# Retention part of a fused kernel: the last tile in another order, and four low parts of the feed-forward made on VectorE ahead of the last block's gating

## What is computed

```python
for i in range(N_LAYERS):                       # 2 layers
    ln_x = layer_norm(x, ln1_g[i], ln1_b[i])
    q, k, v, xo = split(ln_x @ proj_w[i] + proj_b[i])
    ret = (q k^T * decay) v                     # 16 heads of 16, causal
    ret = (ret * silu(xo)) @ reto_w[i] + reto_b[i]
    x = x + ret
    h = layer_norm(x, ln2_g[i], ln2_b[i])
    x = x + gelu(h @ ffn1_w[i] + ffn1_b[i]) @ ffn2_w[i] + ffn2_b[i]
return layer_norm(x, lnf_g, lnf_b)              # then added to the stream before the part
```

## Time and profile before

| what | value |
|---|---|
| median of 3 runs | 1531.19 us |
| the 3 runs | 1527.48, 1531.32, 1531.19 us |
| time of the profiled execution | 1527.78 us |
| its span in the profile | 1525.9 us |
| busy: TensorE, VectorE, ScalarE, GpSimd | 1339.6, 1028.3, 596.3, 648.9 us |
| mean granted clock of TensorE over the span | 0.95 of full speed |

### The profile page before, as it was taken

One profiled execution on the slowest core, in us unless ns is written; L12 is line 12 of the kernel. 1 busy time (PEld: TensorE's weight loads), 2 busy tenths in 40 slices (PEclk: granted clock), 3 DMA queues, 4 the chain that ended last, 5 costly groups with the idle time before them and its releaser, 6 DMA issues. The chain is left out here.

```text
span 1525.9 us, 30606 instructions
## 1 busy us (share of the span) xinstructions
PE 1339.6 (88%) x11824; PEld 1098.0 (72%) x11824; DVE 1028.3 (67%) x2359; ACT 596.3 (39%) x1006; POOL 648.9 (43%) x508
## 2 busy tenths in 40 slices
PE   3899998478999999999998999999998637999993
PEld 2479995267888887887887887887787524699962
DVE  5854664768777777867767777877775377556634
ACT  6335664213343334234344233334333345266630
POOL 4765505524232232424334342543461455755045
PEclk9899999779999999999999999999999868999997
DMA  9987757500000000000010000000000051577544
GB/s 335 360 273 253 242 169 228 177 15 1 2 1 2 1 2 2 1 2 32 12 56 2 1 15 2 16 15 2 15 15 1 14 194 45 186 247 235 189 151 138
DMA packets 109323, 139.18 MB, mean 91 GB/s; under 512 B 11776, under 2 KB 95616, under 8 KB 109184
## 3 DMA queue, kind: packets, MB, share of 16 engines
q1 hardware_dynamic: 94784, 101.56, 20.4%
q0 software_dynamic: 12288, 33.57, 6.6%
q10 hardware_dynamic: 2112, 2.10, 0.4%
HBM read 71.66 MB, written 65.54 MB: 90 GB/s over the span
## 5 line engine op out<-in xcount | busy, mean ns | idle before, releaser
L1603 DVE TENSOR_TENSOR l_probs<-l_banks,l_past 128x512 f32<-128x512 f32 x256 | 159.9, 681 | 33.9 <-PE l_banks L1793 33.6
L1462 POOL TENSOR_TENSOR l_g_lo<-l_q,l_g_hi 128x1024 fp32r<-128x1024 f32 x16 | 53.8, 3361 | 266.3 <-ACT l_g_hi L1377 266.3
L79 PE MATMUL l_w_ps<-l_w_hi,l_f_hi 128*128 128x256 f32 x512 | 152.5, 298 | 15.7 <-DVE l_f_lo L1634 13.9
L1386 ACT ACTIVATE l_act_f<-l_w_ps,l_ffn_b 128x512 f32<-128x512 f32 x128 | 88.2, 689 | 190.6 <-PE l_w_ps L81 184.5
L80 PE MATMUL l_w_ps<-l_w_lo,l_f_hi 128*128 128x256 f32 x512 | 145.8, 285 | 0.0
L81 PE MATMUL l_w_ps<-l_w_hi,l_f_lo 128*128 128x256 f32 x512 | 145.7, 285 | 0.0
L79 PE MATMUL l_w_ps<-l_b_hi,l_w_hi 128*128 128x512 f32 x256 | 110.3, 431 | 13.4 <-POOL l_b_lo L1458 13.4
L79 PEld LDWEIGHTS l_w_ps<-l_w_hi,l_f_hi 128*128 128x128 f32 x512 | 99.0, 193 | 25.2 <-DVE l_f_lo L1634 23.0
L1634 DVE TENSOR_TENSOR l_f_lo<-l_act_f,l_f_hi 128x512 fp32r<-128x512 f32 x128 | 98.6, 818 | 18.1 <-ACT l_f_hi L1387 18.1
L597 POOL DMA_INDIRECT a_picked<-rows,a_pos_i x64 | 64.3, 1005 | 90.8 <-issue 69.5
L81 PE MATMUL l_w_ps<-l_b_hi,l_w_lo 128*128 128x512 f32 x256 | 102.0, 398 | 0.0
(11 more groups left out here) (376 smaller groups left out, 4022.1 us busy)
## 6 DMA issues: line engine op xcount, KB each, us to landing
rows<-a_zeros SPq DMA_DIRECT2D x15, 1024.0 KB, 12.6
a_xb<-rows SPq DMA_DIRECT2D x46, 256.0 KB
rows<-a_yb SPq DMA_DIRECT2D x46, 256.0 KB, 3.1
b_xb<-rows SPq DMA_DIRECT2D x46, 256.0 KB, 3.3
rows<-b_yb SPq DMA_DIRECT2D x46, 256.0 KB, 2.6
a_w_in<-in_moe_w SPq DMA_DIRECT2D x15, 384.0 KB, 12.7
b_w_in<-in_moe_w SPq DMA_DIRECT2D x15, 384.0 KB, 8.4
l_w<-in_ffn_w SPq DMA_DIRECT2D x8, 512.0 KB, 6.9
```

Of the source, the lines that this page charges most:

```text
L79: tensor.matmul(out, w_hi, x_hi, start=start, stop=False)
L1386: nc.scalar.activation(act_f[:, f, :], w_ps[:, f % 2, :], ACT.Gelu, bias=ffn1_b[:, b.layer, f:f + 1]).then_inc(act_done, 1)
L1603: dve.tensor_tensor(probs[c % 2][:, r * w:(r + 1) * w].rearrange("p (h n) -> p h n", n=P), banks[:, r, :].rearrange("p (h n) -> p h n", n= ...
```

## The change

Two things are changed.

First, in every step with a tile before it, block 3 of VectorE makes `f_lo` pieces 3, 4, 5 and 6 before `gate_result`, and only piece 7 behind it.

Second, the end is in another order. In step 15 TensorE does the first of the four groups of `feed_out` before `project_out`, then two groups, `turn_b`, and the last group. VectorE measures and normalises tile 13 before it adds the retention, and makes `b_lo` itself (`low_b` leaves GpSimd's list in this step, where it stood behind `finish` of tile 13). For tile 15 the hidden products go to the `banks` of PSUM and the four groups of `feed_out` to four banks of their own (`w_ps` and `rm_ps`). The tail of tile 15 is then done per block of 128 tokens: `measure_last(s)` and `finish_last(s)`. The final scale, shift and old stream are folded into two operations, for which GpSimd adds the shift to the old stream beforehand (`last_old`, loaded into `xn2` behind `turn_b`).

The diff, cut to its core:

```diff
+        def hidden_ps(b, f):
+            return banks[:, f % 2, :] if b.n == final.n else w_ps[:, f % 2, :]
+
+        def fed_ps(b, s):
+            return (w_ps[:, s, 0:D] if s < 2 else rm_ps[:, s - 2, 0:D]) if b.n == final.n else feed_ps[:, s, :]
@@ sync
-                with sp.Fori(1, NT) as t:
+                for t in range(1, NT - 1):
                     sp.wait_ge(final_done, t)
                     sp.dma_start(x_old[:, :, :], view[t]).then_inc(x_old_in, 16)
+                sp.wait_ge(bT_done, final.n + 1)
+                sp.dma_start(last_old[:, :, :], view[NT - 1]).then_inc(last_old_in, 16)
@@ scalar, step
                         root("f", after(b, -1))
-                        root("f", b)
+                        _, mv, std = norms["f"][:3]
+                        for s in range(SUB):
+                            act.wait_ge(last_var, s + 1)
+                            nc.scalar.activation(std[:, s:s + 1], mv[:, s, 1:2], ACT.Sqrt, bias=eps[:, :]).then_inc(last_std, 1)
...
                     if more == 0:
+                        root("f", after(b, -1))
                         root("2", a)
-                        root("f", after(b, -1))
@@ gpsimd, step
                     if a is None:
+                        pool.wait_ge(last_old_in, 16)
+                        carry(3)
+                        pool.tensor_tensor(last_old[:, :, :], last_old[:, :, :], normf[:, 1:2, :].broadcast_to([P, SUB, D]),
+                                           ALU.add).then_inc(last_old_done, 1)
                         finish(after(b, -1))
...
-                    low_b(a)
+                    if more:
+                        low_b(a)
@@ vector
+                def measure_last(s):
+                    stats, mv = norms["f"][:2]
+                    dve.wait_ge(last_fed, s + 1)
+                    dve.wait_ge(fed, final.n + 1)
+                    link(dve.tensor_tensor(tile_of(final, s), tile_of(final, s), fed_ps(final, s), ALU.add))
+                    dve.memset(carrier[:, 3:4], 0.0)
+                    link(dve.bn_stats(stats[:, s, :], tile_of(final, s)))
+                    dve.memset(carrier[:, 3:4], 0.0)
+                    dve.bn_aggr(mv[:, s, :], stats[:, s, :]).then_inc(last_var, 1)
+
+                def finish_last(s):
+
+                    _, mv, std, rstd = norms["f"][:4]
+                    dve.wait_ge(last_std, s + 1)
+                    dve.wait_ge(last_old_done, 1)
+                    dve.reciprocal(rstd[:, s:s + 1], std[:, s:s + 1]).then_inc(last_step, 1)
+                    stepped[0] += 1
+                    link(dve.scalar_tensor_tensor(tile_of(final, s), tile_of(final, s), mv[:, s, 0:1], normf[:, 0, :],
+                                                  ALU.subtract, ALU.mult))
+                    dve.scalar_tensor_tensor(tile_of(final, s), tile_of(final, s), rstd[:, s:s + 1], last_old[:, s, :],
+                                             ALU.mult, ALU.add).then_inc(final_done, 1)
@@ vector, step
                         normalise_f(after(b, -1))
-                        add_feed(b)
-                        measure_final(b)
+                        for s in range(SUB):
+                            measure_last(s)
+                            if s == 1:
+                                finish_last(0)
+                            if s == 2:
+                                finish_last(1)
+                                finish_last(2)
+                        finish_last(SUB - 1)
...
+                        if b is not None and c == SUB - 1:
+                            for f in FEEDS[c - 1] + FEEDS[c][:1]:
+                                low_feed(b, f)
+                            gate_result(a, c)
+                            continue
                         gate_result(a, c)
...
-                        for f in FEEDS[SUB - 1]:
+                        for f in FEEDS[SUB - 1][1:]:
                             low_feed(b, f)
                     if more == 0:
+                        measure_final(after(b, -1))
+                        normalise_f(after(b, -1))
                         add_retention(a)
                         measure_retained(a)
-                        measure_final(after(b, -1))
                         normalise_2(a)
                         scale_b(a)
-                        normalise_f(after(b, -1))
+                        low_b(a)
                         add_feed(b)
@@ tensor, step
                     if more == 0:
+                        feed_out(b, range(0, 1))
                         project_out(a, last_state)
-                        feed_out(b)
+                        feed_out(b, range(1, 3))
                         turn_b(a)
+                        feed_out(b, range(3, SUB))
                         return
```

More of the change, by code:

```diff
@@ L1272, in retention @@
         added = sem("added")
+        last_old_in, last_old_done, last_fed, last_step, last_var, last_std = (
+            sem("last_old_in"), sem("last_old_done"), sem("last_fed"), sem("last_step"), sem("last_var"), sem("last_std"))
         x_old_in, xf_done, scaled, shifted, final_done = (
@@ L1318, in is_number @@
             return isinstance(a.n, int) and a.n == n
+        final = whole(NL * NT - 1)
+        last_old = xn2
+        def hidden_ps(b, f):
+            return banks[:, f % 2, :] if b.n == final.n else w_ps[:, f % 2, :]
+        def fed_ps(b, s):
+            return (w_ps[:, s, 0:D] if s < 2 else rm_ps[:, s - 2, 0:D]) if b.n == final.n else feed_ps[:, s, :]
         def own_count(kind, a):
@@ L1385, in feed @@
                     act.wait_ge(ffn1_done, KF * b.n + f + 1)
-                    nc.scalar.activation(act_f[:, f, :], w_ps[:, f % 2, :], ACT.Gelu, bias=ffn1_b[:, b.layer, f:f + 1]).then_inc(act_done, 1)
-                    nc.scalar.activation(f_hi[:, f, :], w_ps[:, f % 2, :], ACT.Gelu, bias=ffn1_b[:, b.layer, f:f + 1]).then_inc(f_hi_done, 1)
+                    nc.scalar.activation(act_f[:, f, :], hidden_ps(b, f), ACT.Gelu, bias=ffn1_b[:, b.layer, f:f + 1]).then_inc(act_done, 1)
+                    nc.scalar.activation(f_hi[:, f, :], hidden_ps(b, f), ACT.Gelu, bias=ffn1_b[:, b.layer, f:f + 1]).then_inc(f_hi_done, 1)
                 def step(a):
@@ L1635, in low_feed, with low_b @@
                                       ALU.subtract).then_inc(f_lo_done, 1)
+                def low_b(t):
+                    dve.wait_ge(b_hi_done, t.n + 1)
+                    dve.tensor_tensor(b_lo[:, :, :], full[:, :, :], b_hi[:, :, :].bitcast(F32), ALU.subtract).then_inc(b_lo_done, 1)
                 def add_retention(a):
@@ L1727, in _ @@
                 steps(dve, step)
[L1728 to L1732, removed]
-                                      normf[:, r:r + 1, :].broadcast_to([P, SUB, D]), op).then_inc(xf_done, 1)
-                dve.wait_ge(xf_done, NT + 2)
-                dve.wait_ge(x_old_in, 16 * NT)
-                dve.tensor_tensor(tile_of(last), tile_of(last), x_old[:, :, :], ALU.add).then_inc(added, 1)
             @block.tensor
@@ L1842, in feed_in @@
                         pe.wait_ge(f_hi_done, KF * b.n + f - 1)
-                    elif a is None:
-                        pe.wait_ge(added, b.n)
-                    else:
+                    elif a is not None:
                         pe.wait_ge(v_done, 2 * a.n + f + 1)
@@ L1852, in feed_in, with feed_out @@
                         w = slice(f * P, (f + 1) * P)
-                        last = split3(pe, w_ps[:, f % 2, :], w1_hi[:, k, w], w1_lo[:, k, w], b_hi[:, k, :], b_lo[:, k, :],
+                        last = split3(pe, hidden_ps(b, f), w1_hi[:, k, w], w1_lo[:, k, w], b_hi[:, k, :], b_lo[:, k, :],
                                       k == 0, k == KD - 1)
                     last.then_inc(ffn1_done, 1)
-                def feed_out(b):
+                def feed_out(b, subs=range(SUB)):
                     pe.wait_ge(f_hi_done, KF * (b.n + 1))
@@ L1860, in feed_out @@
                         weights_ready(pe, b.layer, FFN2)
-                    for s in range(SUB):
+                    for s in subs:
                         t = slice(s * P, (s + 1) * P)
@@ L1865, in feed_out @@
                                 pe.wait_ge(f_lo_done, KF * b.n + f + 1)
-                            last = split3(pe, feed_ps[:, s, :], f_hi[:, f, t], f_lo[:, f, t], w2_hi[:, f, :], w2_lo[:, f, :],
+                            last = split3(pe, fed_ps(b, s), f_hi[:, f, t], f_lo[:, f, t], w2_hi[:, f, :], w2_lo[:, f, :],
                                           f == 0, f == KF - 1)
-                    last.then_inc(ffn2_done, 1)
+                        if b.n == final.n:
+                            last.then_inc(last_fed, 1)
+                    if b.n < final.n and s == SUB - 1:
+                        last.then_inc(ffn2_done, 1)
                 def project_out(a, n):
@@ L1887, in step @@
                             feed_in(a, b, f)
+                        pe.wait_ge(added, b.n)
                         feed_out(b)
```

5 lines of the change are left out of this document (added).

## The result

| what | before | after |
|---|---|---|
| median | 1531.22 us (4 runs, 1527.48 to 1531.32) | 1482.57 us (4 runs, 1480.03 to 1486.25) |
| ratio, 95% interval | | 0.9689 [0.9666, 0.9712] |
| profiled execution, its span | 1527.78, 1525.9 us | 1481.23, 1479.1 us |

A forecast was written before the change was run, and what follows sets the result against it. The prediction took TensorE, the busiest engine, as held by waits for f_lo and at the end of the retention part. Terms 22.4 + 0.9 + 22.8 = 46.1 us led from 1527.8 to 1481.7, plus 1.3: 1483.0 us, range 1477 to 1491.

The forecast's parts named there:

- The odd steps: feed_out of seven odd steps: early low pieces end TensorE's f_lo wait and the clock falls, gaining 22.4 us.
- VectorE's idle time ahead of the gating: Sign in block 3 of odd steps: VectorE's idle time before the gating is near 3 us, not 6.
- q_wide: Second layer: two of TensorE's four waits for GpSimd's q_wide go, gaining 0.9 us (0 to 0.9).
- The even steps: Even steps: gating moves back 2.5 us, project_out's cover of 6.6 us hides it, feed_out stays 12.77 us: 0 us.
- The end: From the last retention matmul to the retention part's end: reordered work ends at 1210.4, not 1233.2, gaining 22.8 us.
- the second norm beside `finish`: Before turn_b: GpSimd's finish of tile 13 can hold VectorE's norm; turn_b starts between 1175.1 and 1176.8, taken as 1176.0.
- The tail: Behind the last group: 2.8 us against 8.8 before, beginning at 1206.8; with 0.8 us of GpSimd hold it ends at 1210.4.
- the 9.3 us: Before the hidden layer: its start, 13.35 us behind turn_b before, comes earlier with b_lo on VectorE, worth 9.3 us.
- From the profile to the median: Whole kernel: 46.1 us off the profiled 1527.8 gives 1481.7; 1.3 us added for run spread gives 1483.0.
- The port: Tail: a VectorE operation reading two SBUF operands beside GpSimd lasts as long as GpSimd's; up to 1.3 us, 0.8 taken.

The follow-up runs named there:

- one_ahead: The changed kernel with only piece 3 ahead of the last gating and 4 to 7 behind: 1670.32 us, ratio 0.9812 to the kernel before.
- two_ahead: The changed kernel with pieces 3 and 4 ahead of the last gating and 5 to 7 behind: 1655.07 us, ratio 0.9720 to the kernel before.
- before_state: The changed kernel with pieces 3 to 6 made ahead of the state update too: 1650.38 us, ratio 0.9646 to the kernel before.
- no_finish14: The changed kernel without GpSimd's finish of tile 14, which is stored unfinished: 1661.64 us, ratio 0.9720 to the kernel before.
- end_only: The changed kernel with the low pieces back behind the gating, the end still changed: 1682.20 us, ratio 0.9874 to the kernel before.

## Why the prediction was right

- **The odd steps** (22.4 forecast): the seven stretches went from 103.5 to 80.15 us, 23.4. The step held: pieces early, piece 7 clear of `g_lo`, clock at 1.00. The size is a little off because I took 11.6 for a stretch that is ideally full and lasts 11.45. The cause that I gave, one piece beside `g_lo`, is now shown by `one_ahead` and `two_ahead`. VectorE's idle time ahead of the gating is 1.10 us, and none in steps 7 and 9, not near 3: I took the high parts of the pieces for ready, but they come at ScalarE's pace, one each 1.4 to 1.6 us. The 5.96 us of idle time were room enough even so.
- **`q_wide`** (0.9): two of four waits went, 1.0 us. The time between the stretches, summed over the steps, fell by 2.5 us, so another 1.5 went that I did not name.
- **The even steps** (0): 12.78 to 12.86 against 12.77, right to 0.3 us over all seven. But I looked for a loss only. I had seen VectorE wait ahead of the state update, and `before_state` shows that 12 us lay there.
- **The end** (22.8): 22.2. `project_out` starts 4.2 us behind the retention (4.1 forecast), `turn_b` 14.3 (13.6 forecast, within its bounds 12.7 to 14.4), the hidden layer 19.4 (18.7), the second product 33.0 (32.2), the end 48.6 (48.0). The whole error is the second norm beside `finish`: I took 0.9 of a hold of up to 1.7, and it was nearly all of it. The tail, 4.24 us, was 4.3 in the forecast. `project_out` of before took 4.4 us (1167.03 to 1171.47), not the 4.6 that I wrote; the sum doesn't use it. That GpSimd's order ahead of `b_lo` was most of the 9.3 us is shown: 7.0 by order, 2.7 by engine and clock.
- **From the profile to the median.** The profiled executions differ by 46.6 us, the sum was 46.1. Two unnamed amounts nearly cancel in this: from step 1's `feed_out` to the end of the part 47.7 us went, and 0.9 came back outside, most of it ahead of that `feed_out`. That the two sums agree to 0.5 us is luck by as much. I then added 1.3 us for the spread of the runs of before, which I put down to the clock's falls in odd steps. This reason is wrong: with these falls gone, the runs of after spread over 6.2 us (before 3.8). Where the spread comes from stays open; the clock also falls in the first and third parts, and there not at the same places in different traces. It cost nothing here, by luck.
- **The port.** In the tail both held operations end 0.3 us behind the end of GpSimd's beside them: they were held until it was over. The prediction had such an operation last as long as GpSimd's, 2.4 us; they took 1.71 and 1.55, and 0.47 in `no_finish14`. The Trainium skill (SBUF — State Buffer, the section on the two separate sides) says that whichever of the two starts first keeps the shared port pair for its whole instruction and the other blocks. The tail agrees, and `g_lo` only in part: in the odd steps of before it got in behind one piece (2.85 us), but in all seven even steps it was held through three pieces in a row (4.09 to 4.10). What decides between the two is open.

## What to carry to other kernels

Count from the gating operation which instructions of two engines will lie beside each other, and clear the one that collides: here two pieces of 0.62 us moved ahead gave the odd steps as much as four, because the second cleared the collision. Before an engine's wait for TensorE, ask what of its list is ready already, and look at every such wait of the loop, not only at the one that the change is about. A term that the forecast puts at 0, as that of the even steps, deserves the question what it could still give.

## What was not expected of the hardware

- TensorE's clock fell from 2.4 to 1.2 GHz behind waits of 1.99 us for `f_lo` in nine of fourteen odd steps (four of seven in the kernel before, five of seven in `end_only`), though the wait and its place were the same in all. Behind the 1.65 us of `one_ahead` it fell in none of seven, nor behind the changed kernel's three waits of 1.2 to 1.5; behind a wait of 2.14 it fell in one trace and not in another, and behind 2.33, 3.08, 3.97, 4.15 and 10.46 it did. At the start of the second layer TensorE waits for the state: in nine traces for 2.05 to 2.35 us, each with a fall behind it, in five for 1.05 to 1.76, with none. So a wait of 2 us costs 2 or 3.4, by what these runs don't show. My expectation for `one_ahead` took a wait of 2 us and had a fall of the clock as a possibility; the wait came out shorter.
- Beside GpSimd, VectorE's operations from SBUF to SBUF were held (low pieces 6.51 us for four, the normalisation 3.35 for 1.38), while statistics (0.42) and the additions that read PSUM (0.41) kept their times in the same stretch.
